# Smaller first pieces, later factors and other PSUM banks in a conv-and-routed-experts kernel

## The chip, the cores and the metric
One core of a Trainium2 chip. The metric is the device time of one execution in microseconds (us), the median of several.

## The reference
The input x has 8 batches of 512 tokens with 1024 channels, float32. A depthwise causal convolution of 8 taps (`cond_2048`, with a bias) gives y. Each token of y chooses one of 8 experts, and the chosen expert's 1024 x 1024 matrix is applied to it; x is added.

```python
y = conv1d_causal_depthwise(x, cond_2048) + b          # (8, 512, 1024)
idx = argmax(einsum('bsh,eh->bse', y, w_router), -1)
all_out = einsum('bsh,efh->bsef', y, w_experts)
out = x + take_along_axis(all_out, idx)                # the chosen expert alone
```

## The kernel before
Every engine has an instruction stream written out by hand, with waits on semaphores. There are two phases on TensorE.

**Convolution and logits.** The 4096 tokens are four groups (two batches each). The 1024 channels are 128 sets of 8 channels. A set is one matmul at L814 (two instructions in the trace): the x of the set against a small matrix of taps (`mats`), which gives the convolution of eight phases and the set's share of the router's logits at once. Eight sets are a pack; a group has 16 packs, one 512 KB (later 256 KB) load of x each, into a ring of eight. Seven sets share a PSUM bank, so a group has 19 banks and the whole 76; they rotate over banks 0 to 5 (`CONV_BANKS`). ScalarE evicts a bank with two copies (L437 the logits' part, L438 the rows) and counts it in `conv_out`.

**The start.** The matrices are products of `factors`, loaded in five pieces: pack 0, pack 1, packs 2 and 3, packs 4 to 7, packs 8 to 15. SP issues pieces 0, 3 and 4 among its loads of x; ScalarE issues pieces 1 and 2 on its own queue and then waits for all of the first x (`x_in[0]`) before it asks for the constants (L418). VectorE makes each pack's matrices with two products (L506, L508); pack 0's are made in two pieces of `START_SETS` sets, and the x of pack 0 is also loaded in two pieces (L345, L346), so that TensorE can start on the first. Before that TensorE does 24 dummy matmuls on zeros (L836). Within pack 0, set number `START_SETS` waits for the second pieces.

**Routing.** When a group's logits are complete, VectorE chooses the experts (`choose`, L543 to L552), TensorE counts the tokens ahead of each in its expert (`rank`, L826 and L829, in bank 6 or 7 by the group's parity), VectorE makes the positions (`place_rows`, ends in `pos_ready`), and GpSimd scatters the group's rows to DRAM, sorted by expert (L925). The rank of group g is done in group g + 1 on TensorE; the last one inside the first slot's products.

**Products.** The sorted tokens are worked on in slots of 128. A slot is turned (L689), split in a high and a low half (ScalarE L451, VectorE L694), and takes 48 matmuls of 512 columns at L858: three products of halves, eight chunks, two column halves. Slot 0 needs the expert's weights (`w_first`, split at L446 and L680 during the last group), its tokens' low half (`ys_lo`), and two free banks. Even and odd slots use `out_ps[0]` and `out_ps[1]`: banks 4 and 5, and banks 0 and 1. Slot 0 waits for all evictions but the last four, slot 1 for all. Behind chunk 2 of slot 0 stands `rank(LAST)`, which waits for the last group's chosen experts.

Of the kernel before, what the change touches and what calls it, by code (L numbers as in the profile page):

```python
# [16 lines left out]
BATCH, SEQ, H, TAPS, EXPERTS = 8, 512, 1024, 8, 8  # L17
# [3 lines left out]
GROUPS = BATCH // GROUP  # L21
GT = GROUP * SEQ
TPG = GT // P
# [20 lines left out]
PACK = 8  # L44
# [4 lines left out]
BANKS = -(-SETS // PER_BANK)  # L49
# [5 lines left out]
def bank_sets(n):  # L55
    return range(n * PER_BANK, min((n + 1) * PER_BANK, SETS))
# [5 lines left out]
def on_second_queue(n):  # L62
    return n % 2 == 1 and PACKS + X_RING <= n < GROUPS * PACKS


def sets_done(g, s):
    return g * len(ENDS) + ENDS.index(s) + 1
# [6 lines left out]
LAST = GROUPS - 1  # L74
# [17 lines left out]
N_CONST = C_TOKEN + TILES  # L92
N_FACTORS = CH + SETS * (PHASES + EXPERTS)
FACTOR_PACKS = [(0, 1), (1, 2), (2, 4), (4, 8), (8, PACKS)]
START_SETS = PACK // 2
START_MATMULS = 24


# [66 lines left out]
def build(nc, x_both, x_t, x_rows, factors_t, experts, consts, out):  # L165
    ctx = ExitStack()
    with ctx:  # L167
# [6 lines left out]
        def sem(name):  # L174
            return ctx.enter_context(nc.semaphore(name))
# [53 lines left out]
            return cst[:, at:at + n]  # L229

        ps = ctx.enter_context(nc.psum_tensor("ps", [P, 8, HALF], F32))
        out_banks = [4, 0]
        out_ps = [ps[:, b:b + 2, :].rearrange("p a n -> p (a n)") for b in out_banks]

        def conv_bank(n):
            return ps[:, n % CONV_BANKS, :]

        def rank_ps(g):
            return ps[:, 6 + g % 2, 0:(TPG + 1) * EXPERTS].rearrange("p (t e) -> p t e", t=TPG + 1)

        const_in = sem("const_in")
        factors_in = [sem(f"factors_in{k}") for k in range(len(FACTOR_PACKS))]
# [9 lines left out]
        conv_out = sem("conv_out")  # L252
# [5 lines left out]
        pos_ready = sem("pos_ready")  # L258
# [34 lines left out]
        def load_x(queue, n):  # L293
            s = n % X_RING
            if n >= X_RING:

                queue.wait_ge(conv_mm, pack_done(n - X_RING))
            if n < DOUBLED:
                queue.dma_start(xs[:, s, :, :].rearrange("p c t -> p (c t)"), x_both[n]).then_inc(x_in[s], 16)
            else:  # L300
                side = (1 - n % 2) * SIDE
                queue.dma_start(xs[side:side + SIDE, s, :, :].rearrange("p c t -> p (c t)"), x_t[n - DOUBLED]).then_inc(x_in[s], 16)

        def load_factors(queue, k):
            a, b = FACTOR_PACKS[k]
            cols = slice(0 if k == 0 else CH + a * PACK * (PHASES + EXPERTS), CH + b * PACK * (PHASES + EXPERTS))
            queue.dma_start(factors[:, cols], factors_t[:, cols]).then_inc(factors_in[k], 16)  # L307
# [4 lines left out]
        def _(sp):  # L312
# [31 lines left out]
            load_factors(sp, 0)  # L344
            sp.dma_start(x_0[:, 0:START_SETS * P], x_both[0][:, 0:START_SETS * P]).then_inc(x_start, 16)  # L345
            sp.dma_start(x_0[:, START_SETS * P:], x_both[0][:, START_SETS * P:]).then_inc(x_in[0], 16)  # L346
            load_x(sp, 1)
# [62 lines left out]
        @block.scalar  # L410
        def _(act):
            act.wait_ge(warm_zero, 2)
            nc.scalar.activation(warm[:, 1:2], warm[:, 0:1], ACT.Identity)
            load_factors(act, 1)
            load_factors(act, 2)

            act.wait_ge(x_in[0], 16)
            act.dma_start(cst[:, :], consts).then_inc(const_in, 16)  # L418
            act.wait_ge(empty_ready, 1)
            act.dma_start(y_sorted.rearrange("(e r) n -> r e n", e=EXPERTS)[0:P, :, H:],  # L420
                          empty[:, :].bitcast(F32).unsqueeze(1).to_broadcast([P, EXPERTS, ROW - H])).then_inc(empty_out, 16)

            def evict(g, b):
                n = g * BANKS + b
                if b == 0 and g >= 2:

                    act.wait_ge(y_out[g % 2], TPG * 16)
                if b == 0 and g >= 1:

                    act.wait_ge(most_sum, g)  # L430
                    act.wait_ge(logit_sum, g)
                sets = bank_sets(b)

                act.wait_ge(conv_mm, sets_done(g, sets[-1] + 1))
                m = len(sets)
                to = rows[g % 2][:, :, sets[0] * CH:(sets[0] + m) * CH].rearrange("p j (c i) -> p j c i", i=CH)
                nc.scalar.copy(part[:, :, b], conv_bank(n)[:, PER_BANK * SIDE:]).then_inc(part_out, 1)  # L437
                nc.scalar.copy(to, conv_bank(n)[:, 0:m * SIDE].rearrange("p (c j i) -> p j c i", j=PHASES, i=CH)).then_inc(conv_out, 1)  # L438
                for passed in range(g * PACKS, (g + 1) * PACKS):
                    if sets[0] < (passed % PACKS + 1) * PACK <= sets[-1] + 1 and on_second_queue(passed + X_RING):  # L440
                        load_x(act, passed + X_RING)

            def high(c, raw, arrived, count):

                act.wait_ge(arrived, count)
                nc.scalar.copy(w_sb[:, c, HI, :], raw[:, c, :]).then_inc(w_hi, 1)  # L446

            def high_y(t, k):

                act.wait_ge(y_blocks, t + 1)  # L450
                nc.scalar.copy(ys[k][:, HI, :, :].rearrange("p c s -> p (c s)"),  # L451
                               y_cols[k][:, :, :].rearrange("p c s -> p (c s)")).then_inc(ys_hi, 1)

            def high_w(t):

                new = act.value_load(tab_i[0:1, 2, bass.ds(t, 1)], min_val=0, max_val=2)
                for k in range(2):
                    with act.If(new == k + 1):
                        nth = act.value_load(tab_i[0:1, 1, bass.ds(t, 1)], min_val=1, max_val=EXPERTS - 1)
                        for c in range(HC):  # L460

                            act.wait_ge(gemm_chunk, (t - 1) * HC + (c + 1))
                            high(c, w_raw[k], raw_in[k][c], nth * 8 + 8 * (1 - k))

            for g in range(LAST):
                for b in range(BANKS):
                    evict(g, b)
            ready = [c for c in range(HC)]
            for b in range(BANKS):
                if b == Y_BANK:  # L470

                    act.wait_ge(w_split, 2)
                    high_y(0, 0)
                evict(LAST, b)
                while ready and 2 * PACK * (ready[0] + 1) <= bank_sets(b)[-1] + 1:

                    act.wait_ge(conv_mm, sets_done(LAST, 2 * PACK * (ready[0] + 1)))
                    c = ready.pop(0)
                    high(c, w_first, first_in[c], 16)
            high_y(1, 1)  # L480

            act.wait_ge(gemm_chunk, HC)
            high_y(2, 0)
            high_y(FIRST, FIRST % RING)
            act.wait_ge(table_ready, 1)
            high_w(FIRST)

            last = act.value_load(one_i[0:1, 3:4], min_val=0, max_val=ROUNDS - 1)
            with act.Fori(0, ROUNDS) as i:
                with act.If(i < last + 1):  # L490
                    for k in range(RING):
                        t = i * RING + (FIRST + k)
                        high_y(t + 1, (FIRST + k + 1) % RING)
                        high_w(t + 1)

        @block.vector
        def _(dve):
# [216 lines left out]
            for n in range(PACKS):  # L714
# [3 lines left out]
                if n == 0:  # L718
                    build_mats(0, START_SETS)
                    build_mats(START_SETS, PACK - START_SETS)  # L720
                else:
# [70 lines left out]
        def _(pe):  # L792
            def conv(g, s):
                n, b = g * PACKS + s // PACK, s // PER_BANK
                if s % PACK == 0:
# [6 lines left out]
                    else:  # L802
                        pe.wait_ge(doubled, n - PACKS + 1)
                if g == 0 and s == START_SETS:
                    pe.wait_ge(mats_ready, 2)
# [13 lines left out]
            def rank(g):  # L819

                pe.wait_ge(chosen_ready, g + 1)
                pe.wait_ge(const_in, 16)
                if g >= 2:

                    pe.wait_ge(pos_ready, g - 1)
                nc.tensor.matmul(rank_ps(g)[:, 0:TPG, :], before[:, 0:P], chosen[:, :, :], start=True, stop=False,  # L826
                                 skip_group_check=True)
                for t in range(TPG):
                    mm = nc.tensor.matmul(rank_ps(g)[:, t + 1:, :], before[:, P:],  # L829
                                          chosen[:, t, :].unsqueeze(1).to_broadcast([P, TPG - t, EXPERTS]),  # L830
                                          start=False, stop=(t == TPG - 1), skip_group_check=True)
                mm.then_inc(ranked, 1)
# [44 lines left out]
            def load_of(t):  # L877
                return pe.value_load(tab_i[0:1, 1, bass.ds(t, 1)], min_val=0, max_val=EXPERTS - 1)

            pe.wait_ge(conv_out, GROUPS * BANKS - 4)  # L880
            gemm(0, 0, None)
            pe.wait_ge(conv_out, GROUPS * BANKS)
            gemm(1, 1, True)
# [142 lines left out]
```

## Time and profile before

| | |
|---|---|
| median of 3 runs | 513.11 us (511.46 to 513.98) |
| profiled execution, its own time | 512.61 us |
| its span | 510.8 us |
| TensorE matmuls busy | 502.5 us, 98% |
| VectorE, ScalarE, GpSimd busy | 287.6, 150.5, 133.2 us |
| mean transfer rate | 255 GB/s |

The profiled execution is one run with a hardware profile; its times are counted from the span's start. The time outside the span is 512.61 - 510.8 = 1.8 us. Loads are named by the tile that they write and the tensor that they read.

### The profile page before, as it was taken

What the parts mean: (1) busy time and instruction counts of PE and PEld (TensorE: products, weight loads), DVE (VectorE), ACT (ScalarE), POOL (GpSimd) and SP (SyncE); (2) the same over time, 40 slices, a digit from 0 to 9 for tenths busy, and PEclk for the clock granted to TensorE, in tenths of its full rate; (3) what the DMA queues carried; (4) which work ended last, traced back from release to release, by engine and by line L of the source; (5) the groups of instructions that cost most, each with busy time, mean ns of one, the idle gap of its engine ahead of it and who ended that gap; (6) DMA issues with size and microseconds to landing.
All of it is one profiled execution on the core that took longest, in us unless ns stands there. A gap on an engine that the chain in (4) does not pass through costs nothing.

```text
span 510.8 us, 9483 instructions
## 1 busy us (share of the span) xinstructions
PE 502.5 (98%) x2764; PEld 435.5 (85%) x2765; DVE 287.6 (56%) x418; ACT 150.5 (29%) x255; POOL 133.2 (26%) x148
## 2 busy tenths in 40 slices
PE   8999999999999999999999999999999999999995
PEld 8999999998888888888888888888888888888884
DVE  4947373769885233599753422863266343472961
ACT  2444444286101001365620000610043010340710
POOL 0004325063622111323311312203122322122222
PEclk9999999999999999999999999999999999999998
DMA  8977999999779999699998664695649655534445
GB/s 290 411 221 212 398 282 405 348 346 309 264 253 283 341 350 299 184 348 358 327 395 249 175 198 123 202 372 177 185 133 354 221 165 158 169 116 130 145 142 165
DMA packets 59623, 130.31 MB, mean 255 GB/s; under 512 B 12752, under 2 KB 32720, under 8 KB 59600
## 3 DMA queue, kind: packets, MB, share of 16 engines
q1 hardware_dynamic: 41696, 70.12, 44.3%
q0 software_dynamic: 14832, 54.27, 29.6%
q10 hardware_dynamic: 3072, 5.65, 3.5%
q8 instruction: 10, 0.16, 0.1%
q14 instruction: 13, 0.11, 0.1%
HBM read 94.56 MB, written 35.45 MB: 255 GB/s over the span
## 4 chain that ended last, share of the span: by engine, by line
PE 93%; DMA 5%; issue 0%; POOL 0%; DVE 0%; DVEq 0%; ACT 0%; SPq 0%; POOLq 0%
PE ps L858 75%; PE ps L814 18%; DMA y_sorted<-rows,pos_i 3%; DMA xs<-x_t 2%; DMA xs<-x_both 1%; POOL out L937 0%; DVEq L167 0%; DVE xs L516 0%; PE ps L829 0%; SPq L307 0%; ACT rows L438 0%; ACT part L437 0%; PE ps L826 0%; POOLq L978 0%; DVE x_row L702 0%
## 5 line engine op out<-in xcount | busy, mean ns | idle before, releaser
L858 PE MATMUL ps<-w_sb,ys 128*128 128x512 f32 x1680 | 381.6, 389 | 0.4 <-ACT rows L438 0.4
L858 PEld LDWEIGHTS ps<-w_sb,ys 128*128 128x128 f32 x1680 | 315.2, 188 | 66.1 <-ACT rows L438 0.5
L689 DVE STREAM_TRANSPOSE y_cols<-y_blk 128x1024 f32<-128x1024 f32 x36 | 44.8, 1243 | 140.1 <-PE ps L858 131.6
L814 PE MATMUL ps<-mats,xs 128*128 128x128 f32 x1024 | 117.8, 278 | 1.4 <-DMA xs<-x_both 1.1
L814 PEld LDWEIGHTS ps<-mats,xs 128*128 128x128 f32 x1024 | 116.9, 195 | 1.9 <-DVE mats L508 1.4
L451 ACT CAST ys<-y_cols 128x1024 fp32r<-128x1024 f32 x36 | 37.9, 1052 | 269.4 <-DVE y_cols L689 269.4
L680 DVE TENSOR_TENSOR w_sb<-w_raw,w_sb 128x1024 fp32r<-128x1024 f32 x56 | 64.2, 1218 | 3.3 <-ACT w_sb L446 3.3
L937 POOL DMA_INDIRECT out<-x_row,idx x35 | 40.8, 1165 | 80.3 <-DVE x_row L704 76.4
L944 POOL COPY idx<-ids_all 128x1 int32 (+1 forms) x36 | 15.2, 421 | 173.5 <-DMA out<-x_row,idx 118.7
L446 ACT CAST w_sb<-w_raw 128x1024 fp32r<-128x1024 f32 x56 | 56.4, 1050 | 9.5 <-PE ps L858 8.6
L925 POOL DMA_INDIRECT y_sorted<-rows,pos_i x32 | 35.3, 1103 | 78.1 <-PE ps L814 74.9
L930 POOL DMA_INDIRECT x_row<-x_rows,idx x36 | 38.9, 1080 | 31.0 <-POOL idx L944 29.2
L516 DVE COPY xs<-xs 56x1008 f32<-56x1008 f32 x48 | 33.0, 688 | 24.5 <-DMA xs<-x_t 23.2
L694 DVE TENSOR_TENSOR ys<-y_cols,ys 128x1024 fp32r<-128x1024 f32 x36 | 44.0, 1223 | 0.5 <-ACT ys L451 0.5
L437 ACT COPY part<-ps 128x64 f32<-128x64 f32 x76 | 21.9, 289 | 66.7 <-PE ps L814 55.7
L438 ACT COPY rows<-ps 128x448 f32<-128x448 f32 (+1 forms) x76 | 40.8, 540 | 0.0
L702 DVE TENSOR_TENSOR x_row<-ps,x_row 128x512 f32<-128x512 f32 x35 | 23.2, 663 | 28.1 <-DMA x_row<-x_rows,idx 21.4
L704 DVE TENSOR_TENSOR x_row<-ps,x_row 128x512 f32<-128x512 f32 x35 | 23.6, 675 | 0.0
L506 DVE TENSOR_TENSOR mats<-factors 128x512 f32<-128x512 f32 (+1 forms) x17 | 11.1, 653 | 5.8 <-DMA factors<-factors_t 5.8
L508 DVE TENSOR_TENSOR mats<-factors 128x512 f32<-128x512 f32 (+1 forms) x17 | 11.1, 653 | 0.0
L680 DVE TENSOR_TENSOR w_sb<-w_first,w_sb 128x1024 fp32r<-128x1024 f32 x8 | 9.7, 1224 | 1.1 <-ACT w_sb L446 0.9
L446 ACT CAST w_sb<-w_first 128x1024 fp32r<-128x1024 f32 x8 | 8.5, 1066 | 0.0
(102 smaller groups left out, 47.7 us busy)
## 6 DMA issues: line engine op xcount, KB each, us to landing
w_raw<-experts SPq DMA_DIRECT2D x56, 512.0 KB, 9.5
y_blk<-y_sorted SPq DMA_DIRECT2D x152, 128.0 KB, 3.4
xs<-x_both SPq DMA_DIRECT2D x15, 512.0 KB, 9.8
xs<-x_t SPq DMA_DIRECT2D x28, 256.0 KB, 7.0
xs<-x_t ACTq DMA_DIRECT2D x20, 256.0 KB, 7.5
w_first<-experts SPq DMA_DIRECT2D x8, 512.0 KB, 9.7
ids_all<-y_sorted SPq DMA_DIRECT2D x38, 1.0 KB, 4.5
x_row<-x_rows,idx POOLq DMA_INDIRECT x36, 4.6
```

Of the source, the lines that this page charges most:

```text
L438: nc.scalar.copy(to, conv_bank(n)[:, 0:m * SIDE].rearrange("p (c j i) -> p j c i", j=PHASES, i=CH)).then_inc(conv_out, 1)
L446: nc.scalar.copy(w_sb[:, c, HI, :], raw[:, c, :]).then_inc(w_hi, 1)
L451: nc.scalar.copy(ys[k][:, HI, :, :].rearrange("p c s -> p (c s)"), y_cols[k][:, :, :].rearrange("p c s -> p (c s)")).then_inc(ys_hi, 1)
L516: V.tensor_copy(xs[old:old + USED, s, :, :].rearrange("p c (b t) -> p (c b) t", b=GROUP)[:, :, 1:], xs[new:new + USED, s, :, :].rearrange( ...
L680: V.tensor_tensor(w_sb[:, c, LO, :], raw[:, c, :], w_sb[:, c, HI, :].bitcast(F32), ALU.subtract).then_inc(w_split, 1)
L689: V.transpose(y_cols[k][:, :, :].rearrange("p m (t i) -> p t m i", t=4), y_blk[k][:, :, :, :]).then_inc(y_blocks, 1)
L694: V.tensor_tensor(ys[k][:, LO, :, :].rearrange("p c s -> p (c s)"), y_cols[k][:, :, :].rearrange("p c s -> p (c s)"), ys[k][:, HI, :, :].r ...
L814: mm = nc.tensor.matmul(to, xs[:, n % X_RING, s % PACK, :], mats[:, s, :].rearrange("p (u n) -> p u n", n=SIDE), start=(s == sets[0]), sto ...
L858: return nc.tensor.matmul(out_ps[k][:, f * HALF:(f + 1) * HALF], ys[k][:, a, c, :], w_sb[:, c, b, f * HALF:(f + 1) * HALF], start=(c == 0 ...
L925: G.indirect_dma_start(y_sorted, at(pos_i[:, g, j:j + 1]), rows[g % 2][:, j, :], None, bounds_check=last_row, oob_is_err=False).then_inc(y ...
L930: G.indirect_dma_start(x_row[:, k, :], None, x_rows, at(index), bounds_check=last_token, oob_is_err=False).then_inc(x_got[k], 16)
L937: G.indirect_dma_start(out, at(index), x_row[:, k, :], None, bounds_check=last_token, oob_is_err=False).then_inc(row_out[k], 16)
```

## The change
`START_SETS` goes from four to two: the first x and the first matrices are made of two sets, the second pieces of six. ScalarE asks for pieces 1 and 2 of the factors only once piece 0 has landed. Slot 0, and with it all even slots, use banks 6 and 7; slot 0 waits for the positions of the group before the last, which were read from one of these banks, instead of for evictions. The last group's rank goes to bank 4 and waits for all evictions.

```diff
-START_SETS = PACK // 2
+START_SETS = PACK // 4
...
-        out_banks = [4, 0]
+        out_banks = [6, 0]
...
         def rank_ps(g):
-            return ps[:, 6 + g % 2, 0:(TPG + 1) * EXPERTS].rearrange("p (t e) -> p t e", t=TPG + 1)
+            return ps[:, 6 + g % 2 if g < LAST else 4, 0:(TPG + 1) * EXPERTS].rearrange("p (t e) -> p t e", t=TPG + 1)
...
             nc.scalar.activation(warm[:, 1:2], warm[:, 0:1], ACT.Identity)
+            act.wait_ge(factors_in[0], 16)
             load_factors(act, 1)
             load_factors(act, 2)
...
                 pe.wait_ge(const_in, 16)
-                if g >= 2:
+                if g == LAST:
+                    pe.wait_ge(conv_out, GROUPS * BANKS)
+                elif g >= 2:
                     pe.wait_ge(pos_ready, g - 1)
...
-            pe.wait_ge(conv_out, GROUPS * BANKS - 4)
+            pe.wait_ge(pos_ready, LAST)
             gemm(0, 0, None)
             pe.wait_ge(conv_out, GROUPS * BANKS)
             gemm(1, 1, True)
```

## Rows read from the trace of the kernel before

**Rows 1.** The page: the span, and TensorE's busy time.
```profile
span 510.8 us, 9483 instructions
...
PE 502.5 (98%) x2764; PEld 435.5 (85%) x2765; DVE 287.6 (56%) x418; ACT 150.5 (29%) x255; POOL 133.2 (26%) x148
```

**Rows 2.** The chain in order of time: start us, us, what.
```profile
by line: PE ps L858 74.6%; PE ps L814 18.0%; DMA y_sorted<-rows,pos_i 3.1%; DMA xs<-x_t 1.6%; DMA xs<-x_both 0.7%; issue 0.4%; POOL out L937 0.2%; DVEq L167 0.1%; DVE xs L516 0.1%; PE ps L829 0.1%; SPq L307 0.1%; ACT rows L438 0.1%; ACT par
...
4.86 36.27 PE ps L814 x304
...
84.93 16.04 DMA y_sorted<-rows,pos_i
...
101.01 8.43 DMA xs<-x_t
```

**Rows 3.** Timeline of the first microseconds: start us, us, engine, line, operation.
```profile
0.97 2.74 PE L836 MATMUL ps<-zeros 128*128 128x128 bf16 x24 [0.97 <-DVE warm L500]
0.98 0.90 ACTq L307 DMA_DIRECT2D factors<-factors_t  x2
1.18 0.43 SPq L345 DMA_DIRECT2D xs<-x_both  x1
...
2.71 0.42 DVE L506 TENSOR_TENSOR mats<-factors 128x256 f32<-128x256 f32 x1 [1.78 <-DMA factors<-factors_t]
...
4.06 0.68 DVE L506 TENSOR_TENSOR mats<-factors 128x512 f32<-128x512 f32 x1
...
6.22 0.33 ACTq L418 DMA_DIRECT2D cst<-consts  x1
...
8.22 0.28 ACT L437 COPY part<-ps 128x64 f32<-128x64 f32 x1 [6.01 <-PE ps L814]
...
10.35 0.29 ACT L437 COPY part<-ps 128x64 f32<-128x64 f32 x1 [1.47 <-PE ps L814]
...
12.35 0.78 DVE L508 TENSOR_TENSOR mats<-factors 128x512 f32<-128x512 f32 x1
...
13.48 0.29 ACT L437 COPY part<-ps 128x64 f32<-128x64 f32 x1 [0.91 <-PE ps L814]
```

**Rows 4.** Windows: us, busy time by engine, granted clock, DMA share, GB/s.
```profile
2.00:4.00 2.00, 1.71 (x17) 1.45 (x14) 1.29 (x4) 0.21 (x2) 0.00 (x0) 1.00 0.88 212
...
6.00:8.00 2.00, 2.00 (x12) 2.00 (x11) 1.75 (x3) 0.00 (x0) 0.00 (x0) 1.00 1.03 412
...
30.00:45.00 15.00, 15.00 (x143) 14.99 (x142) 10.15 (x28) 6.19 (x20) 1.12 (x1) 1.00 0.55 153
...
85.00:110.00 25.00, 24.98 (x230) 24.78 (x229) 13.56 (x31) 12.58 (x37) 6.24 (x7) 1.00 1.04 344
```

**Rows 5.** Line L814 in 4 to 12 us: durations in ns, min/median/max.
```profile
L814 PE MATMUL ps<-mats,xs x45: 274/275/550, 4.9 to 11.9; 128*128 128x128 f32 x45
```

**Rows 6.** Timeline of ScalarE in 118 to 128 us.
```profile
118.16 0.55 ACT L438 COPY rows<-ps 128x448 f32<-128x448 f32 x1
```

**Rows 7.** Timeline of VectorE and TensorE in the same stretch.
```profile
122.19 1.23 DVE L694 TENSOR_TENSOR ys<-y_cols,ys 128x1024 fp32r<-128x1024 f32 x1 [0.46 <-ACT ys L451]
...
123.51 4.34 PE L858 MATMUL ps<-w_sb,ys 128*128 128x512 f32 x18 [0.36 <-ACT rows L438]
...
127.46 0.23 DVE L552 TENSOR_TENSOR chosen<-top,cst 128x64 bf16<-128x64 f32 x1
```

**Rows 8.** DMA issues in the first microseconds: KB each, us to landing.
```profile
xs<-x_both SPq DMA_DIRECT2D x1, 256.0 KB, 3.5
...
cst<-consts ACTq DMA_DIRECT2D x1, 142.0 KB, 5.8
...
factors<-factors_t SPq DMA_DIRECT2D x1, 68.0 KB, 2.0
factors<-factors_t ACTq DMA_DIRECT2D x1, 64.0 KB, 3.0
```

**Rows 9.** Timeline of TensorE in 92 to 111 us.
```profile
110.20 1.05 PE L814 MATMUL ps<-mats,xs 128*128 128x128 f32 x7 [0.22 <-DVE xs L516]
```

## Prediction

> **What bounds the kernel now.** I read the page first. TensorE is busy for 502.5 of 510.8 us [rows 1]. The chain that ended last is TensorE nearly throughout: the expert products (L858) carry 74.6% of the span and the convolution (L814) 18.0% [rows 2]. The reader is to see that a stretch is worth reading only if it takes idle or slow time off TensorE. The chain in order of time then gives the places where another engine or a transfer stands in it: the first landing of x ahead of 4.86, a scatter and a load of x around 85 to 110 [rows 2], and the step into the products at 123.5 [rows 7]. The change touches the first and the last.
>
> The start, read in the timeline. Dummy matmuls keep TensorE busy from 0.97 to 3.71, then it waits for x and starts at 4.86 [rows 2, 3]. The first bank of seven sets is evicted at 8.22, the second at 10.35, the fourth at 13.48 [rows 3]. Steady cadence is therefore 3.13/2 = 1.57 us for seven sets, 0.223 each. The first bank took 3.36. The trace prints the granted clock as 1.00 throughout [rows 4], but the matmuls themselves come in two durations, 550 ns and 275 ns [rows 5], so the first ones ran at the lower of the two levels (1.2 GHz) and the later ones at 2.4 GHz. A set at the low level is then about 2 x 0.223 = 0.446: seven make 3.12, and with 0.24 from the last matmul to the eviction that is the 3.36 seen. The second bank took 2.13, or 0.56 over: 0.56/0.223 = 2.5 more slow sets. So 9.5 sets were slow, and the clock rose at 4.86 + 9.5 x 0.446 = 9.1.
>
> The other end, read in the timeline of 116 to 128. The first slot's products start at 123.51, and the row names ScalarE's L438 as the releaser [rows 7]. But the wait in the code is for all 76 evictions except four, and the fifth from the end is the one at 118.16, so the count was reached at 118.16 + 0.55 = 118.7 [rows 6]. What ends at the right moment is VectorE's L694, the low half of the first slot's tokens: 122.19 + 1.23 = 123.42 [rows 7]. It was itself waiting for ScalarE's L451.
>
> **The change, part by part.**
>
> *First piece of x and first matrices, four sets to two.* The piece is 128 KB instead of 256. It is asked for at 1.18 and landed 3.5 us later [rows 3, 8]. The nearest small load, 68 KB of factors, took 2.0 [rows 8]. So it lands between 3.2 and 4.7. The transfers moved 212 GB/s in 2 to 4 [rows 4], and 128 KB (131,072 bytes) at that rate is 0.6 us on top of the factors' landing at 2.7 (0.71 + 2.0, when VectorE's first product starts [rows 3]); with as much again for the skew of the engines, 3.9 at most, I take 3.7. VectorE's products for the matrices, two for each piece, cost 0.42 at 256 elements and 0.68 at 512 [rows 3], by a straight line 0.29 at 128 and 0.55 at 384. The first two sets' are ready at 2.71 + 2 x 0.29 = 3.3, before x; all eight after 2 x 0.29 + 2 x 0.55 = 1.68, as with 4 x 0.42 = 1.68 now, so by 4.4 at the latest. So TensorE starts at about 3.8 instead of 4.86, does two sets in 0.9, and stands at 4.7 until the other six sets have landed. That piece lands at 6.2 now (the constants' load, queued behind a wait for it, is issued at 6.22 [rows 3]), 1.5 behind the first; it is 384 KB instead of 256, with nothing of the factors' 192 KB beside it, so I take 5.0, between 4.4 (the matrices) and 6.2. Pack 0 ends at 5.0 + 6 x 0.446 = 7.7; now it is 4.86 + 8 x 0.446 = 8.4.
>
> *Factors 1 and 2 asked for after factors 0.* ScalarE issued them from 0.98 to 1.88 [rows 3], 0.45 each; now it waits for 2.7 first, so 2.75 and 3.2. Nothing of ScalarE's is late by it: the next things on its queue are the constants (behind x's landing anyway) and the first eviction. Factors 1 took 3.0 to land [rows 8]; 142 KB on the same queue, asked for at 6.22 when the transfers move 412 GB/s, took 5.8 [rows 3, 4, 8]. So factors 1 land between 5.75 and 8.55. SP issues large loads of x meanwhile, so later than now, but the rate is still 212 and not 412 GB/s, so nearer to the low end: I take 6.5. Pack 1's matrices cost 2 x 0.68 = 1.36, ready at 7.9. That is 0.2 behind pack 0's end at 7.7. Factors 2, asked for at 3.2, by the same 3.0 to 5.8 land at 6.2 to 9.0; pack 2's matrices follow pack 1's, at 7.9 + 1.36 = 9.3 at best and 9.0 + 1.36 = 10.4 at worst. Pack 2 is needed now at 8.4 + 1.5 x 0.446 + 6.5 x 0.223 = 10.5, so this costs nothing by itself.
>
> The Trainium skill, *DMA: Bandwidth & Descriptors*, section "Queues, rings and completion order", says that each transfer engine takes turns between the queues of the two issuing engines, a packet from each. By this rule the first x pieces gain from an empty second queue, as I have it, but the late factors then take turns with the large pieces of x; the trace before has nothing that shows it, since the late factors don't occur in it. The rule alone gives no other number; it makes the second rival below more likely.
>
> *What the start is worth.* If the clock rises at 9.1 again, TensorE has by then done 8 + (9.1 - 7.9)/0.446 = 10.7 sets instead of 9.5: 1.2 x 0.223 = 0.3 us. If it rises as long after the start as now (4.24 us, so 8.0), it has done 8.2 by 8.0 and 13.1 by 9.1: 3.6 x 0.223 = 0.8. I take 0.4, nearer to the first, since TensorE stands twice before. The gain has a ceiling: factors 3, which are not moved, give pack 4's matrices at 12.35 + 0.78 = 13.1, and TensorE reaches pack 4 (set 32) about four sets after the end of the bank evicted at 13.48, 13.48 - 0.24 + 0.9 = 14.1 [rows 3]. So no more than 1.0.
>
> *First slot in banks 6 and 7, last rank in bank 4.* The products now wait for the third group's positions (long done) instead of the 72nd eviction (118.7); the real wait, on L694, stays. Worth 0. If it were the evictions after all, 0.36 [rows 7] would be won, but TensorE would stand at the last rank: its 18 products (18 x 0.224 = 4.0) end at 127.5, and it waits for the chosen experts, written at 127.46 + 0.23 = 127.69 [rows 7]. An earlier start only lengthens that wait. The last rank's new wait, for all 76 evictions, is for four more of some 0.55 each on ScalarE behind L451, over by 124 at the latest and so more than three us before it. Worth 0.
>
> *In between.* From 4.86 the convolution waits for nothing until the chain reaches a scatter at 84.93 [rows 2], so a shift passes. From there it hangs on transfers: the scatter takes 16.04, a load of x that ScalarE can issue only behind it takes 8.43 from 101.01, and TensorE waits 0.22 at 110.2 [rows 2, 9]. The transfers are full there, 1.04 of their share, but 0.55 in 30 to 45 [rows 4]; the scatter is issued by TensorE's progress, so I let the shift pass whole.
>
> **Sum.** -0.4 + 0 + 0: the profiled execution took 512.61, span 510.8, so 512.2. It lies 0.5 under the median of 513.11; against the median I forecast **512.7**. A measurement here tells 0.5%, 2.6 us, from no change, and the three runs spread over 2.5.
>
> **Rivals.**
> 1. *No gain arrives* (25%). The late scatter and load at 85 to 110 do not move forward; there is no slack at 110.2, so TensorE waits 0.6 instead of 0.22. Time 513.1. For it: full transfers. Against: the light stretch before.
> 2. *Factors too late, slower* (14%). Factors 1 land at 8.55 as the constants' 5.8 would have it; pack 1's matrices come at 9.9 against 8.4 needed now, 1.5 lost. The clock may then rise later, up to 6 more slow sets, 1.3 more. Time 514.6, up to 515.9. It decides once factors 1 take over 4.3 us (2.75 + 4.3 + 1.36 = 8.4).
> 3. *The clock rises much sooner* (10%). TensorE now hardly stands between the dummies (3.71) and 3.8. If it rose near 6, at least 5 more of the first sets would be fast, 1.1, cut to the ceiling of 1.0. Time 512.1. The Trainium skill, *TensorE: Matmul & The Clock Gate*, Part 1, has sustained activity release the throttle, which speaks for this case; the idle time at 4.7 to 5.0 speaks against.
>
> The forecast itself has 48%; 3% are left for what I don't see, among it a gain over 2.6.
>
> **Range.** Mechanisms give 512.1 to 515.9 on the median; with the spread of the runs shown (1.7 under, 0.9 over the median) the forecast and rivals 1 and 3 lie in 511.0 to 514.0, and the nearer half of rival 2 brings it to 511.0 to 514.8. Faster by over 0.5% needs more than ceiling and the gap ahead of the products together (1.0 + 0.36): 0.05. Slower needs the far end of rival 2 or an unlucky median: 0.08. Same: 0.87.
>
> **What would show it.** First L814 at 3.7 to 4.0, a gap after four matmuls, then on at 5.0; L506 for pack 1 near 6.5, waiting for factors; L437 first at about 8.0, and by the fourth bank 0.3 to 0.5 under 13.48. L858 still starts right behind L694. A first bank evicted before 7.0 means the clock; an idle gap near 8 ahead of L814, released by L508, means the factors. I am wrong if the shift at 13 us is not there at 123.

## The result, and the profile after

| | median (lowest to highest) | against before, 95% interval |
|---|---|---|
| changed kernel, first measurement, 4 runs | 518.11 us (516.63 to 519.11) | 1.0094 [1.0061, 1.0126] |
| the same, measured again, 6 runs | 517.47 us (516.70 to 519.54) | 1.0075 [1.0047, 1.0104] |
| the kernel before beside them | 512.89 (4 runs), 513.34 (23 runs) | |

The change makes the kernel slower by 4 to 5 us. "The same" was forecast, at 512.7, with a range up to 514.8. The profiled execution took 517.31 us, its span is 515.5.

The timeline of the changed kernel's start (start us, us, engine, line, operation; its lines are one to three further down than before), in answer to [rows 3]:

```profile
2.76 0.90 ACTq L307 DMA_DIRECT2D factors<-factors_t  x2
2.76 0.29 DVE L507 TENSOR_TENSOR mats<-factors 128x128 f32<-128x128 f32 x1 [1.83 <-DMA factors<-factors_t]
...
3.73 0.85 PE L815 MATMUL ps<-mats,xs 128*128 128x128 f32 x4
...
4.98 1.58 PE L815 MATMUL ps<-mats,xs 128*128 128x128 f32 x12 [0.40 <-DMA xs<-x_both]
...
6.37 0.28 ACT L438 COPY part<-ps 128x64 f32<-128x64 f32 x1 [4.15 <-PE ps L815]
...
9.21 0.69 DVE L507 TENSOR_TENSOR mats<-factors 128x512 f32<-128x512 f32 x1 [5.02 <-DMA factors<-factors_t]
...
10.56 9.71 PE L815 MATMUL ps<-mats,xs 128*128 128x128 f32 x70 [4.00 <-DVE mats L509]
...
13.23 0.28 ACT L438 COPY part<-ps 128x64 f32<-128x64 f32 x1 [6.20 <-PE ps L815]
...
15.39 0.28 ACT L438 COPY part<-ps 128x64 f32<-128x64 f32 x1 [1.50 <-PE ps L815]
...
16.95 0.28 ACT L438 COPY part<-ps 128x64 f32<-128x64 f32 x1 [0.91 <-PE ps L815]
```

TensorE starts early, as intended, and has pack 0 done at 6.56. Then it stands for 4.00 us: VectorE itself waited 5.02 us for factors 1, which landed at 9.2. In the transfers' view of the first microseconds (KB each, us to landing), in answer to [rows 8], the first x is quick and factors 1 take twice their old time:

```profile
xs<-x_both SPq DMA_DIRECT2D x1, 128.0 KB, 2.4
...
factors<-factors_t ACTq DMA_DIRECT2D x1, 64.0 KB, 6.4
```

The windows (us, TensorE's busy time, granted clock, DMA share, GB/s) show what follows from the pause:

```profile
7.00:9.00 2.00, 0.00 (x0) 1.00 0.95 312
9.00:11.00 2.00, 0.44 (x3) 0.98 0.96 336
11.00:13.00 2.00, 2.00 (x12) 0.50 1.07 412
13.00:15.00 2.00, 2.00 (x14) 0.67 1.05 406
15.00:17.00 2.00, 2.00 (x21) 1.00 1.04 404
```

TensorE did nothing from 6.56 to 10.56; the granted clock then reads 0.50, the 1.2 GHz level, until some way into 13 to 15, and 12 to 14 matmuls fit where 21 do later. The view prints 1.00 for stretches in which the matmuls of the kernel before were slow [rows 4, 5], so a 1.00 at the start is not to be trusted, but a 0.50 is.

Add it up at the fourth eviction: 16.95 against 13.48 [rows 3], 3.47 later. Pack 1 starts at 10.56, against 8.4 before (eight slow sets behind 4.86): 2.1. The reading of 0.50 for all of 11 to 13 and 0.67 over 13 to 15 makes 2 + 1.3 = 3.3 us at the low level, of which half, 1.7, is lost; the kernel before lost 1.5 sets x 0.223 = 0.3 behind pack 0 (it took 0.446 us for a set at the low level and 0.223 at the high one). 2.1 + 1.7 - 0.3 = 3.5.

The step into the products, VectorE's low half and TensorE's start, in answer to [rows 7]:

```profile
125.47 1.23 DVE L695 TENSOR_TENSOR ys<-y_cols,ys 128x1024 fp32r<-128x1024 f32 x1 [0.46 <-ACT ys L452]
```
```profile
126.80 4.36 PE L861 MATMUL ps<-w_sb,ys 128*128 128x512 f32 x18 [0.37 <-issue]
```

It comes 3.3 later than before, again right behind the low half. From there to the end of the span it is 388.7 us against 387.3, the rest of the difference between the two spans. The other traces below have 387.3 to 390.3 there (one has 394.3), whatever the edit, so these 1.4 us are not shown to be the change's.

### The profile page after: what moved, and what is told of

It is laid out like the page before. It is cut to its first block, busy times and chain, and to the rows that moved or that the text cites. A ratio compares the mean times of both kernels' runs of the same rounds, so it can differ in the third digit from the quotient of the medians.

```text
span 515.5 us, 9483 instructions
## 1 busy us (share of the span) xinstructions
PE 503.5 (98%) x2764; PEld 435.0 (84%) x2765; DVE 288.2 (56%) x418; ACT 150.5 (29%) x255; POOL 134.9 (26%) x148
## 4 chain that ended last, share of the span: by engine, by line
PE 84%; DMA 11%; issue 2%; POOL 1%; DVE 1%; SPq 0%; DVEq 0%; POOLq 0%
PE ps L861 61%; PE ps L815 22%; DMA out<-x_row,idx 7%; DMA factors<-factors_t 2%; DMA x_row<-x_rows,idx 2%; POOL idx L947 0%; DMA ids_all<-y_sorted 0%; SPq L287 0%; POOL x_row L933 0%; DVE y_cols L690 0%; DVE ys L695 0%; POOL out L940 0%; SPq L328 0%; PE ps L832 0%; DVEq L167 0%
## 5 line engine op out<-in xcount | busy, mean ns | idle before, releaser
L861 PE MATMUL ps<-w_sb,ys 128*128 128x512 f32 x1680 | 382.4, 389 | 1.2 <-issue 0.6
L861 PEld LDWEIGHTS ps<-w_sb,ys 128*128 128x128 f32 x1680 | 314.8, 188 | 68.1 <-issue 3.0
L947 POOL COPY idx<-ids_all 128x1 int32 (+1 forms) x36 | 16.5, 458 | 181.3 <-DMA out<-x_row,idx 132.7
L940 POOL DMA_INDIRECT out<-x_row,idx x35 | 41.9, 1197 | 71.4 <-DVE x_row L705 66.6
L507 DVE TENSOR_TENSOR mats<-factors 128x512 f32<-128x512 f32 (+2 forms) x17 | 11.1, 654 | 7.2 <-DMA factors<-factors_t 7.2
L509 DVE TENSOR_TENSOR mats<-factors 128x512 f32<-128x512 f32 (+2 forms) x17 | 11.1, 654 | 0.0
```

Of the source, the lines that this page charges most:

```text
L861: return nc.tensor.matmul(out_ps[k][:, f * HALF:(f + 1) * HALF], ys[k][:, a, c, :], w_sb[:, c, b, f * HALF:(f + 1) * HALF], start=(c == 0 ...
L940: G.indirect_dma_start(out, at(index), x_row[:, k, :], None, bounds_check=last_token, oob_is_err=False).then_inc(row_out[k], 16)
```

## Experiments

The theories. **A**: the factors land late because they are asked for behind large loads of x, TensorE stands, and its clock falls. **B**: the start in two steps costs by itself. **C**: banks 6 and 7 slow the products. **D**: a late request is slow whatever else is under way. **E**: the clock plays no part. **F**: the transfers set the first 15 us, and an earlier start only moves the wait. "Before" runs beside each set of kernels on the same chip.

| run | edit | median us | ratio to before, 95% interval | fourth eviction | products start | from there to the end |
|---|---|---|---|---|---|---|
| e1_sets | START_SETS at two | 514.26 | 1.0002 [0.9973, 1.0031] | 14.15 | 124.00 | 388.3 |
| e2_wait | ScalarE's wait | 518.21 | 1.0075 [1.0047, 1.0104] | 18.48 | 128.32 | 389.9 |
| e3_banks | banks | 513.66 | 0.9997 [0.9973, 1.0021] | 13.17 | 126.30 | 389.1 |
| e4_nowait | changed, no wait | 515.36 | 1.0027 [1.0001, 1.0052] | 14.20 | 124.07 | 390.3 |
| e5_hold_x | changed, x of packs 2.. held | 515.49 | 1.0054 [1.0031, 1.0077] | 14.21 | 125.06 | 387.3 |
| e8_hold_all | changed, x of packs 1.. held | 517.32 | 1.0062 [1.0035, 1.0090] | 15.71 | 125.24 | 387.6 |
| e6_dummies | changed, dummy matmuls in the gap | 517.58 | 1.0082 [1.0054, 1.0110] | 15.98 | 127.89 | 388.0 |
| e7_on_sp | changed, factors on SP | 515.57 | 1.0026 [1.0003, 1.0049] | 14.13 | 123.87 | 387.3 |
| e9_after_again | the changed kernel | 517.47 | 1.0075 [1.0047, 1.0104] | 17.37 | 127.52 | 388.4 |
| e10_more_dummies | before, 34 dummies | 514.92 | 1.0017 [0.9991, 1.0043] | 12.43 | 123.56 | 388.4 |
| e11_sets_dummies | two sets, 32 dummies | 515.53 | 1.0026 [1.0002, 1.0049] | 12.75 | 123.04 | 394.3 |

The last three columns are from each kernel's one profiled execution. It need not be near the median: in e5, e7 and e8 it is the fastest run of its kernel, in e2 and e11 the slowest.

**The parts alone.**

```diff
# e1_sets, on the kernel before
-START_SETS = PACK // 2
+START_SETS = PACK // 4
# e2_wait, on the kernel before
+            act.wait_ge(factors_in[0], 16)
             load_factors(act, 1)
# e3_banks: the other lines of the change, without these two
# e4_nowait, on the changed kernel
-            act.wait_ge(factors_in[0], 16)
```

> The kernel before with START_SETS at two alone. Theory A (the loss is the factors' late landing and what it does to the clock): pack 1's matrices are ready long before TensorE needs them, no gap near 7 us; faster than before by 0.5 to 1.5 us, the fourth eviction under 13.48. Theory B (the early start itself costs, because TensorE stands after two sets and the clock suffers): slower by 1 us or more.

> The kernel before with ScalarE's wait ahead of factors 1 and 2 alone. Theory A: factors 1 land at about 9 us as in the changed kernel, TensorE stands until 10.5, and nearly all of the loss is here: slower by 3 us or more. Theory B: factors 1 land in time when the start is the old one, within 1 us of before.

> The kernel before with the first slot's banks and the last rank's bank alone. Theory A: no difference, within 1 us. Theory C (the banks 6 and 7 cost the products, which took 1.4 us longer in the changed kernel): slower by 1 to 2 us, with gaps in the products between 200 and 285 us.

> The changed kernel without ScalarE's wait ahead of factors 1 and 2. Theory A: the whole loss of 5 us goes, 0.5 to 1.5 us faster than before. Theory C: 1 to 2 us slower than the run with START_SETS alone.

The wait alone costs 0.75%, 3.9 us. In its trace TensorE again stands before pack 1, and the granted clock reads 0.50 for two whole stretches and nearly so for a third:

```profile
9.00:11.00 2.00, 0.15 (x1) 0.76 0.98 367
11.00:13.00 2.00, 2.00 (x10) 0.50 1.06 412
13.00:15.00 2.00, 2.00 (x11) 0.50 1.05 404
15.00:17.00 2.00, 2.00 (x12) 0.53 1.06 408
```

The pause here is shorter than the changed kernel's (3.55 us, from 7.30 to 10.85, against 4.00), and the clock costs more. At the high level the 20 sets from pack 1's start to the fourth eviction would take 20 x 0.223 + 0.24 = 4.7 us; they took 18.48 - 10.85 = 7.6, so 2.9 are lost, against 16.95 - 10.56 - 4.7 = 1.7 in the changed kernel.

START_SETS alone shows no gain (its interval allows 0.3% either way), where A wanted 0.5 to 1.5 us, and not B's loss of 1 us or more either; its fourth eviction, at 14.15, is later than before's 13.48, not earlier. With the factors' loads back beside it, the first x lands later, TensorE starts at 4.46 and then waits for the second piece. The banks alone are worth nothing either, within 0.3%, so C falls. Changed kernel without the wait: the loss shrinks from 0.94 or 0.75% to 0.27%. A holds for the main part; what it expected of the gain does not. Whether the last 0.27% is more than spread is open: its interval barely leaves 1, its trace has 3.0 us more than before between the products' start and the end (2.3 of them three waits of TensorE's), and neither of its two parts costs anything alone.

**Why the factors are late.**

```diff
# e5_hold_x, on the changed kernel (SP); e8_hold_all has the wait ahead of load_x(sp, 1)
             load_x(sp, 1)
+            sp.wait_ge(factors_in[1], 16)
             load_x(sp, 2)
```

> The changed kernel with SP waiting for factors 1 ahead of the loads of x for pack 2 and later; pack 1's load stays ahead. Theory A (factors 1 are late because large loads of x that SP issued stand between): factors 1 land within 3 to 5 us of their issue instead of 6.4, pack 1's matrices are ready by about 7.5 to 8, the wait of 4.0 us shrinks under 2. Theory D (a late request is slow by itself, whatever else is asked for): 6 us again, and 5 us slower than before.

> The changed kernel with SP waiting for factors 1 ahead of all loads of x behind pack 0's. Theory A: factors 1 land 2.0 to 3.0 us after their issue at 2.76, pack 1's matrices are ready by 7.2; the x of pack 1, asked for at about 5.5, becomes the last to arrive (near 9). Theory D: 6 us again.

The view of the issues, factors 1 with nothing of x behind pack 0's ahead of them, from e8_hold_all:

```profile
factors<-factors_t ACTq DMA_DIRECT2D x1, 128.0 KB, 2.5
factors<-factors_t SPq DMA_DIRECT2D x1, 68.0 KB, 2.1
factors<-factors_t ACTq DMA_DIRECT2D x1, 64.0 KB, 2.6
```

and from e5_hold_x, with the x of pack 1 ahead:

```profile
factors<-factors_t ACTq DMA_DIRECT2D x1, 64.0 KB, 4.0
```

So 2.6 us with no 512 KB load of x about, 4.0 with one asked for ahead, and 6.4 in the changed kernel, where two are asked for ahead (at 2.13 and 2.6) and more right behind (from 3.1 on): D falls. The changed kernel's queues in 2.8 to 5.6 and in 5.6 to 7.6 us (q1 is SP's, q10 ScalarE's; packets, MB, share) show two parts of the delay:

```profile
q1 hardware_dynamic: 338, 0.95, 97.0%
q10 hardware_dynamic: 1, 0.00, 0.1%
```
```profile
q1 hardware_dynamic: 149, 0.55, 85.3%
q10 hardware_dynamic: 85, 0.04, 8.0%
```

For nearly three microseconds after the request only one of its packets moves, though nothing else has been asked for on its queue; then its packets share the engines with the much larger ones of x. The Trainium skill, *DMA: Bandwidth & Descriptors*, "Queues, rings and completion order", has the engines take turns between the queues, a packet from each; the second fence fits that in its later part alone (44 packets of SP's queue against 3 in 5.6 to 6.2 us, 78 against 74 in 6.6 to 7.6), the first one does not come from it. What holds the first packet back is left open. It came 1.3 us after the request in e8_hold_all, about 2.6 in e5_hold_x and 2.8 here. So the load that is ahead in e5_hold_x costs 1.3 us before the first packet, and the step from 4.0 to 6.4 lies nearly all behind it, in the time of sharing. No run tells apart what the second load ahead and the loads asked for just behind do to it.

Holding x back doesn't pay. In e5_hold_x the wait for pack 1 shrinks to 1.35 us, as A had it, but the held x of pack 2 then costs another:

```profile
8.06 2.05 PE L816 MATMUL ps<-mats,xs 128*128 128x128 f32 x16 [1.35 <-DVE mats L510]
11.25 9.17 PE L816 MATMUL ps<-mats,xs 128*128 128x128 f32 x80 [1.14 <-DMA xs<-x_both]
```

TensorE in e8_hold_all:

```profile
3.72 3.55 PE L816 MATMUL ps<-mats,xs 128*128 128x128 f32 x16
9.35 2.88 PE L816 MATMUL ps<-mats,xs 128*128 128x128 f32 x15 [2.08 <-DVE mats L510]
```

The row names VectorE, whose product for pack 1 had ended at 6.02 + 0.68 = 6.7. The last to arrive was the x of pack 1, asked for at 5.41 and 3.8 us on its way: 9.2. Both holds remain slower than before.

**What the clock costs.**

```diff
# e6_dummies, on the changed kernel
                     elif g == 0:
+                        if n == 1:
+                            for _ in range(60):
+                                nc.tensor.matmul(ps[:, 7, 0:P], zeros[:, :], zeros[:, :], start=True, stop=True, skip_group_check=True)
                         pe.wait_ge(mats_ready, n + 2)
```

> The changed kernel with 60 dummy matmuls on zeros between pack 0 and pack 1, which fill most of the idle 4 us; no other work changes. Theory A (part of the loss is the clock, which fell at about 11 after the idle stretch): the second and third evictions come 1.56 us apart instead of 2.16, about 1.3 us are won on the changed kernel at the same time of landing. Theory E (the clock plays no part, the idle stretch is all): no difference from the changed kernel.

Its windows, in the stretch in which the changed kernel read 0.50:

```profile
11.00:13.00 2.00, 2.00 (x17) 1.00 1.06 407
```

The clock stays. The kernel measured again starts pack 1 at 10.97 and this one at 10.98, the best comparison: fourth evictions at 17.37 and 15.98, so up to there the clock costs 1.4 us, in one trace of each, and E falls for the start. For the whole time E's forecast holds: in the timed runs nothing is left of the 1.4 (1.0082 against 1.0075 and 1.0094). That the clock's part reaches the total is therefore not shown. The trace shows where this execution gave it back:

```profile
114.57 12.95 PE L818 MATMUL ps<-mats,xs 128*128 128x128 f32 x112 [1.80 <-DVE xs L517]
```

That is the place of [rows 9], where TensorE waited 0.22 before, now 1.80. The kernel measured again waited 0.33 there, the changed kernel's first trace nothing, and e3_banks, whose start is the old one, 2.41. One execution of before had made it look settled.

**Could the early start pay?**

```diff
# e7_on_sp: on the changed kernel, ScalarE issues no factors
             load_x(sp, 1)          # becomes:
+            load_factors(sp, 1)
+            load_x(sp, 1)
+            load_factors(sp, 2)
# e10_more_dummies (34), e11_sets_dummies (32, and START_SETS at two), on the kernel before
-START_MATMULS = 24
+START_MATMULS = 34
```

> The changed kernel with factors 1 and 2 issued by SP, in its own order: x of pack 0, factors 1, x of pack 1, factors 2, x of pack 2; no wait. Theory A: the first x lands near 3.7 as in the changed kernel, the clock rises early, factors 1 land near 5.5 and pack 1's matrices are ready near 7, so 1 to 2 us faster than before. Theory F (any start before 4.8 only moves the waiting to the next piece): the same as before within 0.5 us.

> The changed kernel itself, in more rounds. If the loss is the factors' landing and the clock, as the parts say (3.9 us for the wait alone, 1.3 for the other two together), it is 4 to 5 us slower than before, and the trace again has factors 1 land over 6 us after their issue, with TensorE waiting 3 to 4 us for pack 1's matrices.

> The kernel before with 34 dummy matmuls at the start instead of 24, which fill the gap between 3.7 and 4.8 us. Theory A (the idle gap holds the clock back, and the x of pack 1 is there at 8): the clock rises by 7, the second eviction comes 0.5 to 1.5 us earlier, the total 0.5 to 1 us faster. Theory F (the transfers of x set the first 15 us anyway): the second eviction moves, the fourth does not, no difference in total.

> The kernel before with START_SETS at two and 32 dummy matmuls, so that TensorE hardly stands before its first sets. Theory A: faster than START_SETS alone by up to 1 us. Theory F: the same as before within 0.5 us, with a wait for the x of pack 1 or later in place of the one at the start.

TensorE in e7_on_sp, with factors 1 there in 2.9 us and no wait of ScalarE's:

```profile
3.73 0.81 PE L814 MATMUL ps<-mats,xs 128*128 128x128 f32 x4
4.98 1.58 PE L814 MATMUL ps<-mats,xs 128*128 128x128 f32 x12 [0.43 <-DMA xs<-x_both]
8.23 2.02 PE L814 MATMUL ps<-mats,xs 128*128 128x128 f32 x16 [1.68 <-DMA xs<-x_both]
11.18 5.09 PE L814 MATMUL ps<-mats,xs 128*128 128x128 f32 x42 [0.92 <-DVE mats L508]
```

And in e10_more_dummies:

```profile
4.43 1.11 PE L814 MATMUL ps<-mats,xs 128*128 128x128 f32 x8
6.45 10.41 PE L814 MATMUL ps<-mats,xs 128*128 128x128 f32 x88 [0.92 <-DMA xs<-x_both]
17.85 2.36 PE L814 MATMUL ps<-mats,xs 128*128 128x128 f32 x19 [0.99 <-DVE mats L508]
```

Each fast start runs into the next piece: pack 0's second half, then pack 1's x, then the matrices of pack 2 (ready at 11.07 in e7_on_sp). The row at 17.85 names VectorE, but TensorE had then done 4 + 44 = 48 sets and waited for pack 6. Its matrices had been ready since 14.36 + 0.68 = 15.04; its x, asked for at 6.03 by L299, took 11.7 us to land:

```profile
14.36 0.68 DVE L508 TENSOR_TENSOR mats<-factors 128x512 f32<-128x512 f32 x1
```
```profile
DMA to landing us min/median/max: 11.7/11.7/11.7
```

That is 17.7. In the kernel before, the same piece is asked for at 6.06 and takes 10.7, so it is there at 16.8, and TensorE comes to it 20 sets after the 28 of the fourth bank, which end at 13.48 - 0.24 = 13.24: 13.24 + 20 x 0.223 = 17.7. So about 0.9 us is what an earlier start can gain ahead of it. e10_more_dummies is 1.05 us ahead at the fourth eviction, has lost it at pack 6, and starts its products at 123.56, where before does at 123.51. F's idea holds in it, that a transfer of x takes the gain back, but not F's detail: the fourth eviction did move. e7_on_sp and e11_sets_dummies fit neither theory's number. Both are 0.26% slower than before, 1.3 us, with intervals that barely leave 1, where F had the same within 0.5 us. e9_after_again comes out at the low end of what was expected, 0.75% or 3.9 us, with factors 1 at 6.9 us and a wait of 3.83.

e11_sets_dummies gets furthest, 0.5 us ahead at the products' start. Its profiled execution, the slowest of its twelve, is then thrown back by one wait in them:

```profile
278.29 0.69 DVE L702 TENSOR_TENSOR x_row<-ps,x_row 128x512 f32<-128x512 f32 x1 [11.12 <-DMA x_row<-x_rows,idx]
...
280.94 1.64 PE L858 MATMUL ps<-w_sb,ys 128*128 128x512 f32 x3 [4.04 <-DVE ys L694]
```

VectorE works in order: the low half (L694) that TensorE waits for stands behind a residual (L702) that waited 11.12 us for a gather of x rows. The experts' weights (w_raw) were being loaded in the same stretch; that they held up the gather is not shown. The clock fell with the pause, which makes it dearer than its 4 us:

```profile
278.00:286.00 8.00, 5.06 (x12) 0.57 0.38 105
```

Waits among the products, of 0.3 to 2.3 us in sum, are in ten of the other twelve traces, with whichever edit; before's and e5_hold_x's have none. No version measured beats the kernel before.

## Why the prediction was wrong

**The step that failed** is the second of the change's parts, "So factors 1 land between 5.75 and 8.55 ... I take 6.5". They took 6.4 us from the issue (6.9 when measured again, 6.8 with the wait alone), landed at 9.2, and so lay beyond the end that was to bound them, the constants' 5.8 us. The mean rate of the stretch (212 GB/s) was read as a sign of free transfer engines. It was not: the same row has them busy for 0.88 of the time [rows 4]. Two large requests of x, at 2.13 and 2.6, were already ahead and more followed from 3.1 on; the kernel before had its factors in 3.0 us when it asked at 0.98, ahead of them all. The point that the second rival named, 4.3 us from issue to landing, was passed by two.

**The rival** "Factors too late, slower" had mechanism and sign, with a chance of 14%, and two terms too small: 1.5 for the stall, where TensorE came back 2.1 late, and up to 1.3 for the clock, where the dummies' test gives 1.4 and the trace of the wait alone 2.9. The matrices came at 10.5 and not at 9.9, since the landing at 9.2 lay beyond its 8.55. It did not put in that TensorE would be done with pack 0 well before and stand for 4.0 us, not 1.5: the faster start made the pause longer. That the longer pause made the clock's part larger is not shown, since the wait alone had the shorter pause and lost more. At its far end the rival still gives 515.9, where 518.1 and 517.5 were measured; 1.4 us of the trace lie in the products, where no term of the prediction stands.

**The clock.** It did rise early, as the third rival had it: pack 0's last six sets took 1.58 us for 12 matmuls, the fast level. It did not do so every time: of six traces with this start, e6_dummies and e8_hold_all took 3.60 and 3.55 us for all 16, the low level throughout (8 x 0.446 = 3.57). The gain was then lost in the pause, so forecast and third rival both counted something that could not be kept. The ceiling of 1.0 us is near the 0.9 that the x of pack 6 leaves, but by luck, since it looked at pack 4's matrices alone; the waits in e7_on_sp and e10_more_dummies are for the x of packs 0, 1 and 6 and the matrices of pack 2.

**What held.** Start at 3.73 (3.8 forecast), the second piece at 4.98 (5.0), a gap after four matmuls. The banks and the last rank: 0, and alone they gave 0.9997 [0.9973, 1.0021]. The products (now L861) start at 126.80, right behind the low half, which ends at 125.47 + 1.23 = 126.70; so the evictions were not the wait. The shift at the start was there at the products: 3.47 and 3.3.

**The range** left out the slow end because the bounds of one landing came from one row of another load. It also took too small a spread: 29 runs of the kernel before on one chip go from 511.64 to 519.10, not over the 2.5 us of the three shown. Its low end has a slip that decided nothing: the third rival's 512.1 less 1.7 is 510.4, not 511.0.

## What to carry to other kernels

A request that is moved later is priced by what the other queues have been given by then and are given right behind it, not by its old time to landing nor by the rate in that moment. When a part of the start is made faster, list the landing of each next piece and see which one the engine will now stand at; behind a pause the clock can be low and cost more than it had given (1.7 us in two traces here, 2.9 in a third). Where a row names a releaser that had been done for microseconds, look up when the other inputs landed. A wait that looks small in one execution (0.22 us here) was nothing in some of the others and 2.41 in one, so a gain of one microsecond upstream of it can't be counted on.

## What the hardware showed that I had not expected

A 64 KB load took 2.6 us with no 512 KB load of the other queue about, 4.0 with one asked for ahead, and 6.4 with two ahead and more right behind. Its first packet came about 1.3, 2.6 and 2.8 us after the request, with nothing else asked for on its own queue.

After 4.0 us without work the granted clock still read 0.98 over 9 to 11 and then 0.50: it fell when the work had come back already, at 10.56, so the sets behind the pause paid for it. It isn't always so. In e2_wait the reading over 9 to 11 is 0.76, with the work back only at 10.85, so the clock fell inside the pause, and it read 0.53 still over 15 to 17. In e8_hold_all it read 0.50 over 11 to 13, behind a pause of 2.08 us.
